# The two mask matmuls of the windowed attention: from 128 rows each to 64 rows each, in the two halves of the array

## The reference, cut to what matters

```python
mask = (it < jb) | (it > jb + w) | (jb == -1)
sim = jnp.einsum('bhwie,bhwje->bhwij', bq, bk2) * QK_SCALE
sim = jnp.where(mask, -jnp.finfo(sim.dtype).max, sim)
attn = jax.nn.softmax(sim, -1)
out = jnp.einsum('bhwij,bhwje->bhwie', attn, bv2)
```

## Time and profile before

| | us |
|---|---|
| median of 3 executions | 2161.67 |
| lowest and highest of them | 2152.18, 2171.68 |
| the profiled execution, a fourth | 2155.05 |
| its span, from first to last instruction | 2153.2 |
| PE busy in the span | 2009.6 |
| mean granted clock of TensorE, as a share of full speed | 0.961 |

### The profile page before, as it was taken

One profiled execution on the slowest core, in us unless ns is written; L12 is line 12 of the kernel. 1 busy time (PEld: TensorE's weight loads), 2 busy tenths in 40 slices (PEclk: granted clock), 3 DMA queues, 4 the chain that ended last, 5 costly groups with the idle time before them and its releaser, 6 DMA issues. The chain is left out here.

```text
span 2153.2 us, 46766 instructions
## 1 busy us (share of the span) xinstructions
PE 2009.6 (93%) x19016; PEld 1174.0 (55%) x19016; DVE 1530.1 (71%) x1741; ACT 1311.6 (61%) x1857; POOL 988.3 (46%) x715
## 2 busy tenths in 40 slices
PE   5799887769999999999999999999999999999996
PEld 2122122336666666666666666666666666666663
DVE  3889424548777877778777877778777777778762
ACT  3047784436666666667656766667666676666662
POOL 6000002246555655555555655555555555556540
PEclk9579998979999999999999999999999999999997
DMA  4510001025333345334443434433344433343340
GB/s 108 100 34 3 2 1 35 0 72 140 102 97 97 105 119 135 91 89 113 119 118 97 105 104 132 118 86 97 99 125 124 102 106 100 96 111 94 103 106 25
DMA packets 102357, 194.55 MB, mean 90 GB/s; under 512 B 12400, under 2 KB 32368, under 8 KB 102000
## 3 DMA queue, kind: packets, MB, share of 16 engines
q1 hardware_dynamic: 102144, 191.56, 34.0%
HBM read 123.77 MB, written 54.66 MB: 83 GB/s over the span
## 5 line engine op out<-in xcount | busy, mean ns | idle before, releaser
L1212 POOL TENSOR_TENSOR l_rot<-l_rot,l_rot_s 128x1024 f32<-128x1024 f32 x192 | 455.1, 2370 | 1.0 <-DVE l_rot_s L1540 1.0
L1201 POOL COPY l_kb<-l_kb 128x512 f32<-128x512 f32 x95 | 62.9, 662 | 693.1 <-ACT l_kb L1427 693.1
L1215 POOL TENSOR_TENSOR l_rot<-l_rot,l_norms 128x1024 f32<-128x1024 f32 x192 | 365.2, 1902 | 15.1
L1528 DVE TENSOR_TENSOR l_rot<-ps,l_tab_c 128x1024 f32<-128x1024 f32 x192 | 235.2, 1225 | 173.3 <-ACT l_sq L1401 173.3
L1401 ACT ACTIVATE l_sq<-ps 128x1024 f32<-128x1024 f32 x192 | 196.9, 1025 | 227.2 <-PE ps L1239 224.6
L1540 DVE TENSOR_TENSOR l_rot_s<-ps,l_tab_s 128x512 f32<-128x512 f32 x384 | 245.6, 681 | 0.0
L1519 DVE TENSOR_REDUCE l_norms<-l_sq 128x16 f32<-128x1024 f32 x192 | 232.2, 1209 | 0.0
L1239 PE MATMUL ps<-l_wqkv,xsT 128*128 128x512 f32 x384 | 188.3, 615 | 26.8 <-ACT l_v_tok L1393 15.5
L1427 ACT ACTIVATE l_kb<-ps 64x1024 f32<-64x1024 f32 x192 | 195.8, 1020 | 1.1
L468 ACT ACTIVATE probs<-ps 128x512 f32<-128x512 f32 x256 | 131.9, 605 | 102.8 <-PE ps L419 102.8
L1290 PE MATMUL ps<-l_vb,l_pT 128*32 128x128 f32 x6144 | 188.3, 274 | 1.6 <-ACT l_pT L1393 1.4
(11 more groups left out here) (165 smaller groups left out, 3352.1 us busy)
## 6 DMA issues: line engine op xcount, KB each, us to landing
l_vb<-v_scratch SPq DMA_DIRECT2D x336, 256.0 KB, 4.5
v_scratch<-l_v_tok SPq DMA_DIRECT2D x96, 512.0 KB, 4.8
l_vb<-v_scratch SPq DMA_DIRECT2D x48, 192.0 KB, 3.2
xsT<-xT SPq DMA_DIRECT2D x48, 135.8 KB, 2.5
stack<-scratch SPq DMA_DIRECT2D x96, 64.0 KB
l_xf<-xT SPq DMA_DIRECT2D x48, 128.0 KB, 2.4
l_wqkv_odd<-wqkv SPq DMA_DIRECT2D x9, 512.0 KB, 6.1
scratch<-parts SPq DMA_DIRECT2D x4, 768.0 KB, 11.3
```

Source lines behind the costliest of these rows:

```text
L1212: nc.gpsimd.tensor_tensor(rot[:, t % 2, n], rot[:, t % 2, n], rot_s[:, n], ALU.add).then_inc(added, 1)
L1215: nc.gpsimd.tensor_tensor(rot[:, t % 2, n], rot[:, t % 2, n], norms[:, t % 2, n, :, None].broadcast_to([P, HEADS, DH]), ALU.mult).then_inc ...
L1528: nc.vector.tensor_tensor(rot[:, t % 2, 1 - r], slot(name, t).rearrange("p n (h d) -> p (n h) d", d=DH), tab_c[:, 1 - r, t % TILES, None, ...
```

## The change

The two mask matmuls of a tile use 64 rows each: the one for the slot's first bank takes partitions 0 to 63 of `mask_sel` and `mask`, the one for the second bank takes partitions 64 to 127. The host now lays the 64 rows of both constants out twice. VectorE casts all 128 partitions, the two memsets are gone, and the waits on `consts_set` count 3 in place of 5.

```diff
--- before.py
+++ after.py
@@ -1255,12 +1255,13 @@
                     wait_free(pe, "kT", t)
                     wait(pe, carried, t)
                     if t == 0:
-                        pe.wait_ge(consts_set, 5)
+                        pe.wait_ge(consts_set, 3)
                     take(pe, "s", t)
                     dst = slot("s", t)
                     opening = int(t % TILES == 0)
                     for n in range(2):
-                        nc.tensor.matmul(dst[:, n, :], mask_sel[:, opening, :], mask[:, :], start=True, stop=False,
+                        rows = slice(64 * n, 64 * n + 64)
+                        nc.tensor.matmul(dst[:, n, :], mask_sel[rows, opening, :], mask[rows, :], start=True, stop=False,
                                          skip_group_check=True)
                     for c in range(PAIRS):
                         for j in range(WINDOWS):
@@ -1406,7 +1407,7 @@
                     part = 2 * t + r
                     wait(act, bounded, part + 1)
                     if part == 0:
-                        act.wait_ge(consts_set, 5)
+                        act.wait_ge(consts_set, 3)
                     nc.scalar.activation(norms[:, t % 2, 1 - r], norms[:, t % 2, 1 - r], ACT.Ln, scale=65536.0)\
                         .then_inc(logged, 1)
                     wait(act, logged, part + 1)
@@ -1504,11 +1505,8 @@
             @block.vector
             def _(dve):
 
-                nc.vector.memset(mask[2 * WINDOW:, :], 0.0).then_inc(consts_set, 1)
-                nc.vector.memset(mask_sel[2 * WINDOW:, :, :], 0.0).then_inc(consts_set, 1)
-                nc.vector.tensor_copy(mask[0:2 * WINDOW, :], const("wmask")[0:2 * WINDOW, :]).then_inc(consts_set, 1)
-                nc.vector.tensor_copy(mask_sel[0:2 * WINDOW, :, :],
-                                      const("wsel")[0:2 * WINDOW, :].rearrange("p (a q) -> p a q", a=2))\
+                nc.vector.tensor_copy(mask[:, :], const("wmask")).then_inc(consts_set, 1)
+                nc.vector.tensor_copy(mask_sel[:, :, :], const("wsel").rearrange("p (a q) -> p a q", a=2))\
                     .then_inc(consts_set, 1)
 
                 def sum_squares(t, r):
@@ -1682,11 +1680,13 @@
         bad = (key < r) | (key > r + WINDOW)
         m[r] = np.where(bad, -1e30, 0.0)
         m[WINDOW + r] = np.where(bad | (key < WINDOW), -1e30, 0.0)
+    m[2 * WINDOW:] = m[:2 * WINDOW]
     put("wmask", m)
     s = np.zeros((P, 2, P))
     for q in range(P):
         s[q % WINDOW, 0, q] = 1.0
         s[q % WINDOW + (WINDOW if q < WINDOW else 0), 1, q] = 1.0
+    s[2 * WINDOW:] = s[:2 * WINDOW]
     put("wsel", s)
     return c
```

## The result

The changed kernel takes 2147.78 us (median of 22 executions) beside 2156.16 us for the kernel before (also 22). The ratio is 0.9947, 95% interval 0.9921 to 0.9973: 0.5% faster, some 11 us. The forecast was 0.6%, 12.8 us. Executions of most kernels here lie in two groups some 15 us apart, with the mean granted clock (for the change 0.960 to 0.964, or 0.947 to 0.956), and one of the changed kernel took 6427.25 us, which the ratio leaves out (without it the median is 2143.75). So the layers are compared in the traces as well, beside the ratios: their clock is 1.00, but for their first 35 us and the last few.

The account below looks back on a forecast made before the run. The prediction took the layers to be bound by PE; 72 x 0.110 + 24 x 0.203 = 12.8 us off the 2161.7 us median gave 2148.9 us, with a range from 2137 to 2163 us.

Parts of the forecast that it names:

- What bounds the kernel: Layers: PE, busy 93% of 2153.2 us, sets the end; 0.110 us saved per non-waiting tile, 0.203 per waiting one.
- The pair: Two mask matmuls on array halves run side by side, costing one pass and saving 0.206 us a tile.
- The second switch: Ahead of the masks, going from 128 rows to 64 costs 0.098 us, taken between bounds of nothing and 0.098.
- rival A: Ahead of the masks, rows change at no cost: 19.8 us saved, 2141.9 us; chance 0.13.
- 24 tiles with a wait: Where PE already waits before the masks, the added shape change hides in that wait: 0.203 us saved each.
- Nothing lost elsewhere: ScalarE's copies of keys and values keep up (margins 1.33 and 0.22 us), so no saving counts as lost.
- rival B: In later work PE waits for ScalarE or GpSimd and the gain is swallowed: 2161.7 us, no change; chance 0.11.
- Set-up: Casts at 436 to 438 us keep their durations, at most 0.9 us more, under 30 us of cover: no cost.
- The sum: Over 96 tiles, 72 x 0.110 + 24 x 0.203 = 12.8 us saved.
- The median: Whole execution: three earlier runs' median 2161.67 us less 12.8 gives 2148.9 us, a gain of 0.6%.

Follow-up runs that it names:

- doubled pair: The changed kernel with its two 64-row mask matmuls issued twice; ratio to the kernel before 1.0023, layers 1669.4 us.
- pair in one half: The changed kernel with both mask matmuls on partitions 0 to 63; ratio to the kernel before 1.0033, layers 1667.0 us.
- the change of shape alone: The kernel before with one 64-row matmul of 8 columns added ahead of the two 128-row masks; ratio to the kernel before 1.0078.
- 32 rows: The changed kernel with 32 rows per mask matmul in the 72 tiles that do not open a sequence; ratio to the kernel before 0.9966.
- masks in 128x32: The kernel before with each mask matmul cut into four of 32 weight columns; ratio to the kernel before 0.9963.
- masks in 64x32: The changed kernel with each 64-row mask matmul cut into four of 32 weight columns; ratio to the kernel before 0.9944, layers 1655.3 us.
- values' projection early: The changed kernel with the values' projection ahead of the masks on PE in steps without a mean; ratio to the kernel before 0.9927.

## Why the prediction was right

*What bounds the kernel.* That time off PE comes off the end held for the 0.110 and 0.203 us of the change. Tile by tile, between first scores matmuls, the four distances of a batch went from 15.485, 20.633, 14.410 and 18.245 us to 15.374, 20.524, 14.300 and 18.046: 0.111, 0.109, 0.110 and 0.199 less, where 0.110 three times and 0.203 stood in the forecast.

*The pair.* 0.206 was forecast. The starts are 0.002 to 0.007 us apart, and 0.525 became 0.320. The doubled pair and the pair in one half show the cause.

*The second switch.* Taken as 0.098 between bounds of 0 and 0.098; measured 0.098 (median of the 72 tiles). It is the one step in which I chose, and rival A falls on it. The Trainium skill ("TensorEngine Tiling (Array Packing)", section Key Properties) says that a change of the tiling mode drains TensorE. The traces agree for a change of rows alone too, with this 0.098, which the trace of before could not show.

*24 tiles with a wait.* The gap hides in it, as forecast: 0.195 us before and 0.194 after.

*Nothing lost elsewhere.* Right for this amount, and partly for the wrong reason. In the hidden layer's step ScalarE's margin of 0.22 us went to 0.12. PE's wait for the values' copy stayed at 22 cases of 0.41 us. The view from 540 us on shows 23 and 10.1 us for the earlier trace rows 22 and 8.9, because the last of six longer waits at the start of the layers falls at 540.3 in this trace and at 533.0, outside the view, in that of before:

```profile
  PE ps L1314: 43.6, 72
...
  PE ps L1239: 10.1, 23
```

The nearer limit was another, and the prediction doesn't name it. The run without masks shows it at the copy of the turned probabilities, in the first tile of a batch. There the changed kernel has 0.27 - 0.145 = 0.13 us left, so rival B becomes true for what is saved beyond that.

*Set-up.* The two casts took 0.43 and 1.35 us, for 1.04 and 0.28 before; they didn't keep their durations, as was assumed, but stayed inside the bound of 0.9 us more, 30 us ahead of the first mask.

*The sum.* 12.8 us were forecast. 24 batches times 0.53 are 12.7, and the stretch from the last matmul ahead of the masks to the scores is indeed 12.7 us shorter over the 96 tiles. But the layers became only 11.0 us shorter (11.6 in the second trace), and the ratio says 11. Where the clock is full throughout, from the third batch's scores to the last batch's, 21 batches took 1445.7 us before and 1436.1 and 1436.3 after, 9.5 us less for 21 x 0.53 = 11.1. The term that is missing, 1.6 us, is the last section's.

*The median.* That it came out at 2147.78, 1.1 us from the forecast 2148.9, is luck. The forecast stood on a median of 2161.67 for three executions of the kernel before. Over 22 it is 2156.16, from which the same gain would give 2143.4. What tests the forecast is the gain: 12.8 us beside the 11 of the ratio.

## What to carry to other kernels

Price a packing of the array by starts, not by lengths: here a pair of halves saves one pass (0.21 us for 512 columns), and each added change of shape costs 0.10 us, so a packing wants to save more than its own entry, and its entry belongs where PE waits anyway. Before counting on a larger saving at the same place, look for every copy that the next dense stretch waits for, not only for the wait that shows today. The number of rows in use cost nothing by itself.

## What was not expected: pauses at every so many instructions

In the changed kernel PE stops now and then in the middle of a tile's values, though nothing there waits for an engine. PE in order of time:

```profile
1969.77 1.06 PE L1291 MATMUL ps<-l_vb,l_pT 128*32 128x128 f32 x32
1971.12 0.64 PE L1291 MATMUL ps<-l_vb,l_pT 128*32 128x128 f32 x16 [0.29 <-issue]
```

From 1970.56 to 1971.12 no matmul starts. A view of the DMAs of that moment, from 1967.6 to 1970.2 us, has one packet only, of instructions, which the trace puts at 1968.69:

```profile
DMA packets 1, 0.02 MB, mean 6 GB/s; under 512 B 0, under 2 KB 0, under 8 KB 0
...
q8 instruction: 1, 0.02, 2.3%
```

I numbered PE's instructions in the trace (loads, matmuls, semaphores). Taking distances of over 0.16 us between the starts of two matmuls within the values' line, without those of the last tile, during which the clock is at its lower level in some traces:

| kernel | pauses | sum beyond the usual 0.1, us |
|---|---|---|
| before | 2 | 0.5 |
| both masks in one half | 3 | 0.4 |
| the pair twice | 2 | 0.4 |
| the change of shape alone | 2 | 0.3 |
| the change | 8 | 1.8 |
| the change again | 7 | 2.0 |
| the change, shifted by 64 instructions | 7 | 2.5 |
| 32 rows | 7 | 1.9 |
| masks in 128x32 | 9 | 2.6 |
| masks in 64x32 | 8 | 3.7 |
| no mask | 9 | 3.6 |
| values' projection early | 0 | 0 |

Each of them in this table stands after 194 or 195 of 256 instructions (for the change of shape alone once the matmul record that its trace lacks in every tile is added). The change repeated has six of the eight positions again and one other, with other lengths, up to 0.84 us for the one at 1970:

```profile
1958.84 1.06 PE L1291 MATMUL ps<-l_vb,l_pT 128*32 128x128 f32 x32
1960.46 0.75 PE L1291 MATMUL ps<-l_vb,l_pT 128*32 128x128 f32 x20 [0.57 <-issue]
```

It is after the 32nd matmul record of the same tile again. With 64 instructions more ahead of the layers there are seven pauses (the longest 0.99 us), again at 194 or 195 of 256, and none after the same matmul as in the change. Six are in other tiles. The seventh is in the same tile, 64 instructions earlier: after 24 matmul records of the values, where it was after 56:

```profile
1494.45 0.84 PE L1291 MATMUL ps<-l_vb,l_pT 128*32 128x128 f32 x24
1496.01 0.75 PE L1291 MATMUL ps<-l_vb,l_pT 128*32 128x128 f32 x20 [0.72 <-issue]
```

So it is not the tile but the place in the instruction stream. The changed kernel's trace has 152 transfers of 16 KB in the instruction queue for PE's 39,050 instructions, one for every 256, and kernels with more or fewer instructions have them in the same proportion (157 for 40,202, 151 for 38,666). Scores and values are 256 loads and matmuls in 3.4 us.

What this costs is read from all of the values' matmuls, with steps too small for the table. In the 21 batches with full clock they take 1.6 us more in the change than before. That is how the two masks' 0.53 us a batch came out as 0.46 over the layers (11.0 / 24), and it is most of the 64x32 version's loss.

That the pauses belong to the block boundary is shown by the shift. That PE waits there for the block itself is an inference, but the traces bear it out: each of the table's 64 pauses ends 2.16 to 2.9 us after the start of a transfer, and of 1,519 block boundaries in the layers of these traces none is crossed between 1.7 and 2.16 us after one. Why a transfer begins too late in some tiles isn't shown. The order of the table suggests that a shorter mask or more instructions for the same work bring it about, and the version with the projection moved, the fastest, has none.
